# Two reorderings in a graph network kernel: carried sums fetched three blocks ahead, and edge products made between two count batches

## The chip, the cores and the metric

The kernel runs on one core of one Trainium2 chip. The metric is device time in microseconds (us) of one execution, all stages in one launch. The five engines are PE (TensorE), DVE (VectorE), ACT (ScalarE), POOL (GpSimd) and SP (SyncE); here POOL does nearly nothing but issue indirect DMAs (gathers), and SP issues the plain ones.

## The reference

A two-layer graph network over 12,500 nodes and 400,000 edges (sorted by target), cut to what matters:

```python
# first layer
msg = relu(concat([x[dst], x[src], edge_attr, u[dst]]) @ W1 + b1)
agg = segment_sum(msg, dst)
x   = layernorm(x + relu(concat([x, agg, u]) @ W2 + b2))
# second layer, run twice, with a batch norm behind each run
h   = h0 @ W + b                      # per node
msg = h[src] + edge_attr @ We + be    # per edge
h   = batchnorm(relu(segment_sum(msg, dst) + h) + bias)
x   = layernorm(x + h)
```

The second layer's sum over edges is done as a dense product: for blocks of edges the kernel first counts how often each source node occurs (a matrix of counts, `adj`, kept in HBM), and multiplies these counts by the node values.

## The kernel before, in words

**Edge part** (about 165 to 4605 us of the span). The 400,000 edges are 3125 tiles of 128, five tiles to a step, 625 steps. Sixteen steps are a cycle; cycles 2 to 38 of the 39 whole ones also build the count matrices. Each engine runs its own written-out order of a cycle in a loop; semaphores tie them. In step j of a cycle:

- POOL gathers, in `gather_step` (L703), five times 128 rows of `b_tab` (the source's share of the message) into `rows`, which holds eight steps. Five times a cycle it also gathers target rows, `gather_target` (L690). So there are 85 gathers in a cycle.
- PE makes the **edge products** in `before_add` (L835, L836), two f32 matmuls for the step two ahead, into one of two PSUM halves. It waits for `added` of the step that used this half, which is step j.
- DVE adds the products to the gathered rows: `add_step` (L1402). It waits for the products and for the five gathers. SP then stores the rows to `q_tab`.
- DVE makes the one-hot operands of two **count batches**, before and after the add: `make_hot` (L1411, two instructions each). `make_hot` may start when the batch before the last one is done (`built`).
- PE multiplies them in `build_batches` (L852): 16 matmuls for d = 0, 16 for d = 1. ACT copies the counts to SBUF (L1127, `kept`).
- In steps 1, 4, 7, 10 and 13 DVE also runs the **window terms** of one block of 128 windows of 16 edges, `window_terms` (L1416, L1417, L1419; both inputs in SBUF, f32). In the step behind (2, 5, 8, 11, 14) PE sums such a block in two halves of eight matmuls each, `over_turn` (L877), and in the step behind that DVE scans it (L1455).

**Node part** (about 4605 to 5160 us). For each of 98 blocks of 128 nodes POOL gathers a window of edge rows (`gather_window`, L739, five buffers) and one row of carried sums for each node (`gather_carry`, L747). DVE works the window off in `node_term` (L1416, L1417, L1419, and L1425 that ends it), PE sums it in `node_sum` (L936). Seven blocks are a group; `node_sums` (L1532) adds the carried sums, and waits for all seven carried gathers of its group and for PE's seven sums. POOL's window for block b + 5 waits for PE's sum of block b.

**Second layer** (about 5160 to 7700 us): PE multiplies counts by node values (L998), twice, then a short end.

Of the kernel before, what the change touches and what calls it, by code (L numbers as in the profile page):

```python
# [7 lines left out]
STEPS = TILES // S  # L8
NB = -(-N // P)
# [28 lines left out]
CYCLE = 16  # L38
# [2 lines left out]
BUILD = AP_ // 2  # L41
HOT = 8
WIN = 5
BATCH = 4
PAIR_BATCHES = P // BATCH
QH = NB // 2

def build(nc, a, out):
# [3 lines left out]
    with ctx:  # L52
# [127 lines left out]
        a_node = arena(0, (NB, F))  # L180
        win = arena(25088, (WIN, WM, W0))
        at = 50176
# [98 lines left out]
        carried_on = sem("carried_on")  # L281
        win_got = [sem(f"win_got{u}") for u in range(WIN)]
        a_w_in = [sem(f"a_w_in{n}") for n in range(MC)]
# [369 lines left out]
        def _(pool):  # L653
# [16 lines left out]
            for g in range(NG):  # L670
                if g >= 2:
                    pool.wait_ge(rows_compared, g - 1)
                for q in range(GB):
                    b = g * GB + q
# [61 lines left out]
            def gather_window(b):  # L736
                u = b % WIN
                wait(pool, node_summed, b - WIN + 1 if b >= WIN else 0)
                nc.gpsimd.indirect_dma_start(  # L739
# [3 lines left out]
            def gather_carry(b):  # L743
                g, q = b // GB, b % GB
                if g >= 2 and q == 0:
                    pool.wait_ge(agg_made, g - 1)
                nc.gpsimd.indirect_dma_start(  # L747
                    m_carry_in[:, g % 2, q, :], None, m_carry[:, :],
                    bass.IndirectOffsetOnAxis(ap=m_carried[:, b:b + 1], axis=0)).then_inc(m_carry_in_s[g % 2], 16)

            for b in range(WIN):
                gather_window(b)
            pool.wait_ge(m_carry_out, 16 * MOB)
            for b in range(NB):
                gather_carry(b)
                if b + WIN < NB:
                    gather_window(b + WIN)

            for l in range(2):
                pool.wait_ge(a_carry_out[l], 16 * AOP)  # L760
                for i in range(NB // 2):
                    wait(pool, cat_made, i + l * (NB // 2))
                    for h in range(2):
                        b = 2 * i + h
# [11 lines left out]
        def _(pe):  # L776
# [49 lines left out]
            def before_add(c, j):  # L826
                uu, k = j // 2, j % 2
                us, half = uu % 4, k
                m = c * CYCLE + j
                use = c * 2 + uu // 4  # L830
                wait(pe, added, m - 1)
                if k == 0:
                    pe.wait_ge(eat_in[us], use * 16 + 16)
                pe.nop(nofuse=True)
                mm(psum[:, half, 2 * W0:5 * W0], eat[:, us, 1 - k, 0, :], w_edge[:, :], start=True, stop=True)  # L835
                mm(psum[:, half, 0:2 * W0], eat[0:2 * C, us, 1 - k, 1, :], w_edge[0:2 * C, W0:3 * W0], start=True, stop=True)\  # L836
                    .then_inc(pre_done, 1)

            def build_batches(c, j):
                for d in range(2):  # L840
                    n = j * 2 + d
                    s = (c - 1) * (2 * CYCLE) + n
                    pe.wait_ge(hot_made, s + 1)
                    for b in range(2):
                        r = s * 2 + b
                        bank = 2 + 2 * b
                        wait(pe, kept, r * 2 - 2)
                        pe.nop(nofuse=True)
                        for e in range(BATCH):
                            for h in range(2):  # L850
                                at = slice(h * HALF, (h + 1) * HALF)
                                one = mm(psum[:, bank + h, e * NB:(e + 1) * NB], hot_lo[at, d, b * BATCH + e, :],  # L852
                                         hot_hi[at, d, b * BATCH + e, :], start=True, stop=True)
                        one.then_inc(built, 1)
                    over_turn_at(c, j, d)

            def turn_codes():
# [28 lines left out]
            def over_turn_at(c, j, part):  # L886
                if j in (2, 5):
                    if not (isinstance(c, int) and c == 0):
                        over_turn(c * MC - 2 + j // 5, 3 + j // 5, part)
                elif j in (8, 11, 14):  # L890
                    over_turn(c * MC + (j - 8) // 3, (j - 8) // 3, part)
# [10 lines left out]

            def tile_cycle(c, build_now):
                for j in range(CYCLE):
                    if isinstance(c, int) and c * CYCLE + j + 2 >= STEPS:
                        pass
                    elif j + 2 < CYCLE:
                        before_add(c, j + 2)
                    else:
                        before_add(c + 1, j + 2 - CYCLE)  # L910
                    if isinstance(c, int) and c == 0 and j == 8:
                        turn_codes()
                    if build_now:
                        build_batches(c, j)
                    else:
                        over_turn_at(c, j, 0)
                        over_turn_at(c, j, 1)
                    over_back_at(c, j)
# [163 lines left out]
        def _(act):  # L1082
# [33 lines left out]
            def keep_batches(c, j):  # L1116
                for d in range(2):
                    s = (c - 1) * (2 * CYCLE) + (j * 2 + d)
                    for b in range(2):
                        r = s * 2 + b  # L1120
                        at = j * 4 + d * 2 + b
                        h2, column = at // PAIR_BATCHES, at % PAIR_BATCHES * BATCH
                        if column == 0 and not (isinstance(c, int) and c == 1):
# [641 lines left out]
```

## Time and profile before

| | |
|---|---|
| median of the runs before | 7802.66 us (3 runs, 7797.47 to 7810.06) |
| time of the profiled execution | 7799.23 us |
| its span, first to last instruction | 7797.5 us |
| busy in the span | PE 77%, DVE 57%, ACT 27%, POOL 51% |
| mean granted TensorE clock | 0.765 of full speed |
| HBM traffic | 271 GB/s over the span |

The profiled execution's own time is 1.7 us longer than its span, and 3.4 us under the median. How the rows further down are read: a row of a stretch has its bounds, its length, then the busy time of PE, PEld (weight loads), DVE, ACT and POOL, each with its number of instructions, the granted clock, the DMA share and GB/s. A row of a group has the number of instructions, then busy us and mean ns of one, then the engine's idle us just before them and what ended it ("issue": nothing that the profile shows). A row of a waits view has us in total, times and the longest. A row in order of time has start and length in us, and in brackets the idle time before it.

The share of busy time is a mean over stages that have different limits, so the stages have to be looked at one by one: the edge part is more than half of the time, and the change touches it and the node part, not the second layer.

### The profile page before, as it was taken

What the parts mean: (1) busy time and instruction counts of PE and PEld (TensorE: products, weight loads), DVE (VectorE), ACT (ScalarE), POOL (GpSimd) and SP (SyncE); (2) the same over time, 40 slices, a digit from 0 to 9 for tenths busy, and PEclk for the clock granted to TensorE, in tenths of its full rate; (3) what the DMA queues carried; (4) which work ended last, traced back from release to release, by engine and by line L of the source; (5) the groups of instructions that cost most, each with busy time, mean ns of one, the idle gap of its engine ahead of it and who ended that gap; (6) DMA issues with size and microseconds to landing.
All of it is one profiled execution on the core that took longest, in us unless ns stands there. A gap on an engine that the chain in (4) does not pass through costs nothing.

```text
span 7797.5 us, 166429 instructions
## 1 busy us (share of the span) xinstructions
PE 6012.8 (77%) x60257; PEld 5159.6 (66%) x60257; DVE 4425.6 (57%) x5943; ACT 2114.4 (27%) x5348; POOL 3965.5 (51%) x3933
## 2 busy tenths in 40 slices
PE   3177777777777777777777756689999999999996
PEld 3055555555555555555555546679999999999996
DVE  4168888888888888888888848840011111011113
ACT  1044444444444444444444400000000000000001
POOL 7777777777777777777777764410011110001111
PEclk7576666666666666666666666689999999999998
DMA  5157777777777777777777774569999998999996
GB/s 141 49 175 241 249 237 249 246 253 243 241 257 239 249 241 243 257 245 248 240 248 245 253 221 160 162 257 381 362 382 382 383 381 345 381 363 381 384 380 245
DMA packets 973999, 2113.94 MB, mean 271 GB/s; under 512 B 668085, under 2 KB 759691, under 8 KB 860003
## 3 DMA queue, kind: packets, MB, share of 16 engines
q1 hardware_dynamic: 809823, 1841.27, 63.4%
q0 software_dynamic: 136064, 258.22, 13.6%
q10 hardware_dynamic: 28030, 13.36, 0.9%
q8 instruction: 51, 0.84, 0.0%
q14 instruction: 31, 0.25, 0.0%
HBM read 1457.70 MB, written 654.73 MB: 271 GB/s over the span
## 4 chain that ended last, share of the span: by engine, by line
PE 48%; DVE 20%; issue 12%; DMA 10%; POOL 7%; DVEq 1%; SPq 1%; ACTq 0%; ACT 0%; POOLq 0%
PE psum L998 25%; PE psum L877 10%; DVE edge_area L1411 9%; POOL arena L703 5%; PE psum L852 4%; DMA arena<-adj 4%; PE psum L835 4%; PE psum L836 2%; DVE arena L1402 2%; DMA arena<-b_tab,arena 2%; DMA arena<-in_src_steps 2%; DVE edge_area L1416 1%; DVE arena L1419 1%; DVE arena L1416 1%; POOL arena L717 1%
## 5 line engine op out<-in xcount | busy, mean ns | idle before, releaser
L703 POOL DMA_INDIRECT arena<-b_tab,arena x3125 | 3116.1, 997 | 952.6 <-issue 936.4
L1411 DVE TENSOR_TENSOR edge_area<-psum,arena 128x1024 bf16<-128x1024 f32 x2368 | 2487.4, 1092 | 625.0 <-PE psum L852 624.9
L1127 ACT CAST arena<-psum 128x392 bf16<-128x392 f32 x4736 | 1921.0, 505 | 2113.8 <-PE psum L852 2088.0
L998 PE MATMUL psum<-arena 128*128 128x192 bf16 x29008 | 2446.0, 246 | 29.2 <-DMA arena<-adj 20.9
L998 PEld LDWEIGHTS psum<-arena 128*128 128x128 bf16 x29008 | 2400.5, 98 | 38.0 <-issue 35.2
L852 PE MATMUL psum<-edge_area 64*128 64x98 bf16 x18944 | 1226.1, 241 | 464.8 <-ACT arena L1127 456.9
L765 POOL DMA_INDIRECT arena<-a_carry,a_carried x196 | 185.4, 946 | 2397.3 <-DVE arena L1629 1386.6
L835 PE MATMUL psum<-w_edge,arena 96*128 96x288 f32 x1250 | 677.3, 638 | 885.2 <-DVE arena L1402 885.2
L852 PEld LDWEIGHTS psum<-edge_area 64*128 64x128 bf16 x18944 | 782.3, 110 | 711.3 <-issue 683.1
L1595 DVE TENSOR_REDUCE arena<-psum 128x64 f32<-128x192 f32 x296 | 104.2, 352 | 1698.0 <-PE psum L998 1112.6
L835 PEld LDWEIGHTS psum<-w_edge,arena 96*128 96x128 f32 x1250 | 268.7, 268 | 962.3 <-issue 962.3
L877 PE MATMUL psum<-ident,edge_area 128*96 128x128 f32 x3744 | 648.2, 346 | 1.3 <-ACT arena L1132 0.8
L877 PEld LDWEIGHTS psum<-ident,edge_area 128*96 128x96 f32 x3744 | 595.7, 219 | 28.9 <-issue 3.4
L836 PE MATMUL psum<-w_edge,arena 64*128 64x192 f32 x1250 | 547.2, 533 | 0.0
L836 PEld LDWEIGHTS psum<-w_edge,arena 64*128 64x128 f32 x1250 | 271.9, 270 | 397.9 <-issue 397.9
L1213 ACT COPY arena<-psum 98x256 f32<-98x256 f32 x98 | 36.5, 373 | 1622.2 <-PE psum L1022 1622.2
L1402 DVE TENSOR_TENSOR arena<-psum,arena 128x480 f32<-128x480 f32 x625 | 404.7, 648 | 112.8 <-DMA arena<-b_tab,arena 112.6
L877 PE MATMUL psum<-ident,over_area 128*96 128x128 f32 x2528 | 445.6, 350 | 8.4 <-DVE over_area L1419 6.9
L936 PE MATMUL psum<-arena,ident 128*128 128x96 f32 x1568 | 291.0, 363 | 182.3 <-DVE arena L1425 182.1
L877 PEld LDWEIGHTS psum<-ident,over_area 128*96 128x96 f32 x2528 | 407.6, 222 | 27.4 <-issue 10.1
L936 PEld LDWEIGHTS psum<-arena,ident 128*128 128x128 f32 x1568 | 275.0, 272 | 196.6 <-DVE arena L1425 107.4
L1204 ACT COPY arena<-psum 128x128 f32<-128x128 f32 x50 | 13.3, 266 | 890.2 <-PE psum L1015 890.2
(248 smaller groups left out, 3185.3 us busy)
## 6 DMA issues: line engine op xcount, KB each, us to landing
arena<-adj SPq DMA_DIRECT2D x592, 1568.0 KB, 8.8
adj<-arena SPq DMA_DIRECT2D x296, 1568.0 KB
q_tab<-arena SPq DMA_DIRECT2D x312, 480.0 KB
edge_area<-q_tab SPq DMA_DIRECT2D x117, 768.0 KB
arena<-in_edge_t_steps SPq DMA_DIRECT2D x312, 192.0 KB
over_area<-q_tab SPq DMA_DIRECT2D x78, 768.0 KB
arena<-b_tab,arena POOLq DMA_INDIRECT x3125
over_area<-m_cont SPq DMA_DIRECT2D x196, 48.0 KB
```

The source lines that it names most:

```text
L703: nc.gpsimd.indirect_dma_start(rows[:, us, k, S - 1 - s, :], None, b_tab[:, :], bass.IndirectOffsetOnAxis(ap=index[:, us, 1 - k, s:s + 1], ...
L765: nc.gpsimd.indirect_dma_start(a_carry_in[:, h, :], None, a_carry[l][:, :], bass.IndirectOffsetOnAxis(ap=a_carried[:, b:b + 1], axis=0)).t ...
L835: mm(psum[:, half, 2 * W0:5 * W0], eat[:, us, 1 - k, 0, :], w_edge[:, :], start=True, stop=True)
L836: mm(psum[:, half, 0:2 * W0], eat[0:2 * C, us, 1 - k, 1, :], w_edge[0:2 * C, W0:3 * W0], start=True, stop=True)\
L852: one = mm(psum[:, bank + h, e * NB:(e + 1) * NB], hot_lo[at, d, b * BATCH + e, :], hot_hi[at, d, b * BATCH + e, :], start=True, stop=True)
L877: one = mm(psum[0:W0, 7, 0:P], over_win[n % 2][:, i, :], ident[:, :], start=(i == 0), stop=(i == WM - 1))
L936: one = mm(wide_ps(g % 2)[:, q * P:q * P + W0], ident[:, :], win[:, b % WIN, i, :], start=(i == 0), stop=(i == WM // 2 - 1))
L998: one = mm(psum[:, h, 0:3 * F], ring[:, r, n, :], xs[l][:, k, :], start=(k == 0 and not own), stop=(k == NB - 1))
L1127: copy(stage[:, h2, h, :, column:column + BATCH], psum[:, 2 + 2 * b + h, 0:BATCH * NB].rearrange("p (e n) -> p n e", n=NB)).then_inc(kept, 1)
L1402: V.tensor_tensor(of, psum[:, k, 0:S * W0], of, ALU.add).then_inc(added, 1)
L1411: one = V.tensor_tensor(to[:, d, :, :], over(lanes, [P, HOT, n], 1), over(code, [P, HOT, n], 2), ALU.is_equal)
L1416: V.tensor_tensor(of, of, over(target, [P, WM, F], 1), ALU.add).then_inc(targeted, 1)
```

## The change: what it does

Two edits. On POOL, the carried sums of the first three blocks are gathered at once, and from then on the gather of block b + 3 stands where that of block b stood. On PE, in cycles that build counts, the edge products for the step two ahead are made behind the first count batch, instead of ahead of both. What each instruction computes is the same, and so is their number.

```diff
+AHEAD = 3
...
             pool.wait_ge(m_carry_out, 16 * MOB)
+            for b in range(AHEAD):
+                gather_carry(b)
             for b in range(NB):
-                gather_carry(b)
+                if b + AHEAD < NB:
+                    gather_carry(b + AHEAD)
                 if b + WIN < NB:
                     gather_window(b + WIN)
...
+            def edge_products_ahead(c, j):
+                if isinstance(c, int) and c * CYCLE + j + 2 >= STEPS:
+                    pass
+                elif j + 2 < CYCLE:
+                    before_add(c, j + 2)
+                else:
+                    before_add(c + 1, j + 2 - CYCLE)
...
             def build_batches(c, j):
                 for d in range(2):
...
                         one.then_inc(built, 1)
+                    if d == 0:
+                        edge_products_ahead(c, j)
                     over_turn_at(c, j, d)
...
             def tile_cycle(c, build_now):
                 for j in range(CYCLE):
-                    if isinstance(c, int) and c * CYCLE + j + 2 >= STEPS:
-                        pass
-                    elif j + 2 < CYCLE:
-                        before_add(c, j + 2)
-                    else:
-                        before_add(c + 1, j + 2 - CYCLE)
+                    if not build_now:
+                        edge_products_ahead(c, j)
```

On PE, step 5 of a cycle that builds counts (`w_edge,arena` are the edge products, `psum<-edge_area` of 128x98 a count batch, `ident,edge_area` the first half of a window sum), before:

```order
L835 MATMUL psum<-w_edge,arena 128x288 [waits added]
L836 MATMUL psum<-w_edge,arena 128x192
L852 MATMUL psum<-edge_area 128x98 [waits hot_made,kept]
L852 MATMUL psum<-edge_area 128x98 x7
L852 MATMUL psum<-edge_area 128x98 [waits kept]
L852 MATMUL psum<-edge_area 128x98 x7
L877 MATMUL psum<-ident,edge_area 96x128 [waits m_back_kept,masked,relued]
L877 MATMUL psum<-ident,edge_area 96x128 x7
L852 MATMUL psum<-edge_area 128x98 [waits hot_made,kept]
L852 MATMUL psum<-edge_area 128x98 x7
```

The same step with the change (its lines are numbered 4 to 14 higher):

```order
L864 MATMUL psum<-edge_area 128x98 [waits hot_made,kept]
L864 MATMUL psum<-edge_area 128x98 x7
L864 MATMUL psum<-edge_area 128x98 [waits kept]
L864 MATMUL psum<-edge_area 128x98 x7
L839 MATMUL psum<-w_edge,arena 128x288 [waits added]
L840 MATMUL psum<-w_edge,arena 128x192
L891 MATMUL psum<-ident,edge_area 96x128 [waits m_back_kept,masked,relued]
L891 MATMUL psum<-ident,edge_area 96x128 x7
L864 MATMUL psum<-edge_area 128x98 [waits hot_made,kept]
L864 MATMUL psum<-edge_area 128x98 x7
```

The first count batch no longer stands behind the wait for `added`; the edge products now stand behind it and ahead of the window sum.

On POOL, the beginning of the node part (`m_window` are windows, `m_carried` carried sums), before:

```order
L739 DMA arena<-q_tab,m_window 128x1536 x4
L747 DMA arena<-m_carry,m_carried 128x96 [waits m_carry_out]
L739 DMA arena<-q_tab,m_window 128x1536 [waits node_summed]
L747 DMA arena<-m_carry,m_carried 128x96
L739 DMA arena<-q_tab,m_window 128x1536 [waits node_summed]
```

With the change:

```order
L740 DMA arena<-q_tab,m_window 128x1536 x4
L748 DMA arena<-m_carry,m_carried 128x96 [waits m_carry_out]
L748 DMA arena<-m_carry,m_carried 128x96 x3
L740 DMA arena<-q_tab,m_window 128x1536 [waits node_summed]
L748 DMA arena<-m_carry,m_carried 128x96
L740 DMA arena<-q_tab,m_window 128x1536 [waits node_summed]
```

Three more carried gathers stand ahead of the window of block 5; behind that the two kinds alternate as before, the carried ones three blocks on.

## Rows read from the trace of the kernel before

**Rows 1.** Busy time by engine (x instructions) in a stretch of the edge part.
```profile
2000.00:3000.00 1000.00, 727.36 (x6789) 539.05 (x6787) 843.40 (x972) 482.78 (x1221) 762.85 (x778) 0.66 0.76 246
```
**Rows 2.** Groups of instructions on POOL, 950 to 4500 us.
```profile
L703 POOL DMA_INDIRECT arena<-b_tab,arena x2602 | 2556.7, 983 | 793.1 <-issue 778.2 <-DMA arena<-in_src_steps 14.9
```

**Rows 3.** The same view, 511 to 840 us.
```profile
L703 POOL DMA_INDIRECT arena<-b_tab,arena x239 | 239.0, 1000 | 72.8 <-issue 72.5 <-DMA arena<-in_src_steps 0.3
```

**Rows 4.** The same view, 4490 to 4601 us.
```profile
L703 POOL DMA_INDIRECT arena<-b_tab,arena x79 | 79.9, 1012 | 24.1 <-issue 23.8 <-DMA arena<-in_src_steps 0.3
```

**Rows 5.** Waits of DVE, 950 to 4500 us: us in total, times, longest.
```profile
DVE edge_area L1411 <- PE psum L852: 551.1, 519, 1.5
DVE arena L1402 <- DMA arena<-b_tab,arena: 6.2, 1, 6.2
```

**Rows 6.** The same view, 4490 to 4601 us.
```profile
DVE arena L1402 <- DMA arena<-b_tab,arena: 66.9, 15, 10.7
```

**Rows 7.** Instructions of POOL in order of time, 2010 to 2018 us (start, length).
```profile
2011.27 0.94 POOL L703 DMA_INDIRECT arena<-b_tab,arena  x1 [0.30 <-issue]
2012.52 1.16 POOL L703 DMA_INDIRECT arena<-b_tab,arena  x1 [0.30 <-issue]
2013.98 1.44 POOL L703 DMA_INDIRECT arena<-b_tab,arena  x1 [0.30 <-issue]
```

**Rows 8.** Instructions of DVE in order of time, 2007 to 2040 us.
```profile
2011.65 1.22 DVE L1416 TENSOR_TENSOR edge_area<-edge_area,arena 128x1024 f32<-128x1024 f32 x1
...
2016.53 0.65 DVE L1402 TENSOR_TENSOR arena<-psum,arena 128x480 f32<-128x480 f32 x1
...
2020.37 2.11 DVE L1411 TENSOR_TENSOR edge_area<-psum,arena 128x1024 bf16<-128x1024 f32 x2 [1.17 <-PE psum L852]
...
2024.43 2.10 DVE L1411 TENSOR_TENSOR edge_area<-psum,arena 128x1024 bf16<-128x1024 f32 x2 [1.40 <-PE psum L852]
...
2027.72 2.11 DVE L1411 TENSOR_TENSOR edge_area<-psum,arena 128x1024 bf16<-128x1024 f32 x2 [0.61 <-PE psum L852]
...
2032.32 1.21 DVE L1416 TENSOR_TENSOR edge_area<-edge_area,arena 128x1024 f32<-128x1024 f32 x1
```

**Rows 9.** Matmuls of PE in order of time, 2014 to 2030 us.
```profile
2017.33 1.30 PE L835 MATMUL psum<-w_edge,arena 96*128 96x288 f32 x2 [2.30 <-DVE arena L1402]
...
2020.14 3.67 PE L877 MATMUL psum<-ident,edge_area 128*96 128x128 f32 x16
2023.75 0.53 PE L852 MATMUL psum<-edge_area 64*128 64x98 bf16 x16
...
2026.04 0.65 PE L835 MATMUL psum<-w_edge,arena 96*128 96x288 f32 x2
```

**Rows 10.** Instructions of POOL in order of time, 676 to 682 us.
```profile
676.72 1.99 POOL L703 DMA_INDIRECT arena<-b_tab,arena  x1 [0.30 <-issue]
679.01 1.43 POOL L703 DMA_INDIRECT arena<-b_tab,arena  x1 [0.30 <-issue]
```

**Rows 11.** Instructions of DVE in order of time, 676 to 682 us.
```profile
676.67 1.22 DVE L1416 TENSOR_TENSOR over_area<-over_area,arena 128x1024 f32<-128x1024 f32 x1
```

**Rows 12.** Instructions of POOL in order of time, 2098 to 2104 us.
```profile
2101.26 1.43 POOL L703 DMA_INDIRECT arena<-b_tab,arena  x1 [0.31 <-issue]
```

**Rows 13.** Instructions of DVE in order of time, 2098 to 2104 us.
```profile
2100.00 1.26 DVE L1416 TENSOR_TENSOR over_area<-over_area,arena 128x1024 f32<-128x1024 f32 x1
```

**Rows 14.** Waits of DVE in the node part, 4636 to 5150 us.
```profile
DVE edge_area L1532 <- DMA arena<-m_carry,m_carried: 65.2, 13, 9.8
DVE edge_area L1532 <- PE psum L936: 3.4, 1, 3.4
```

**Rows 15.** Instructions of POOL in order of time, 4630 to 4650 us.
```profile
4631.38 1.34 POOL L747 DMA_INDIRECT arena<-m_carry,m_carried  x1 [16.01 <-DMA m_carry<-over_area]
4633.03 1.88 POOL L739 DMA_INDIRECT arena<-q_tab,m_window  x1 [0.30 <-PE psum L936]
```

**Rows 16.** Instructions of DVE in order of time, 4636 to 4660 us.
```profile
4639.01 1.23 DVE L1416 TENSOR_TENSOR arena<-arena 128x1024 f32<-128x1024 f32 x1 [2.11 <-DMA arena<-q_tab,m_window]
```

## The prediction, made before the changed kernel was run

> **What bounds the kernel now.** I read the busy time by stretches first, then the groups on POOL and the waits of DVE in each part, then the order of time. In the edge part PE and DVE are the busiest engines, 727 and 843 of 1000 us, and POOL shows 763 [rows 1]. The reader should look at POOL's idle time next: between 950 and 4500 us its 2602 gathers were busy 2556.7 us and idle 793.1 us, and all that idle time ended by "issue" or by an index load that was there in time [rows 2]. That is 0.30 us before each gather, in the row of each of them [rows 7]. So POOL gathers without a pause: (2556.7 + 793.1) / 2602 = 1.287 us each. The five target gathers of a cycle take 1.25 us, the distance of two undisturbed ones (2011.27 to 2012.52) [rows 7]. A cycle of 80 + 5 gathers thus takes 103.0 + 6.25 = 109.2 us on POOL, with nothing left over.
>
> DVE looks bound by PE: 519 waits for a count batch, 551 us, and a single wait for gathered rows [rows 5]. Both readings hold, because the two are coupled. An undisturbed gather takes 1.25 us, and 85 of them 106.25 us; the other 3.0 us of a cycle are gathers that DVE stretches. With window terms from 2011.65 on [rows 8] the gathers of 2012.52 and 2013.98 took 1.16 and 1.44 us instead of 0.94 to 0.95 [rows 7]: 0.70 us. How much it costs hangs on where in a gather the terms begin. At 0.38 us behind a gather's start it was that 0.70. At 1.25 us behind the last but one gather (terms at 2100.00 [rows 13], gather at 2101.26 [rows 12]) a single gather took 1.43, which is 0.49 more. With a start at 676.67 [rows 11], just ahead of the gather of 676.72, that one took 1.99 and the next 1.43 [rows 10]: 1.04 + 0.49 = 1.53 us. So each of five window terms in a cycle costs POOL between 0.49 and 1.53 us, now 3.0 / 5 = 0.60. POOL cannot go under 106.25 + 5 x 0.49 = 108.7 us for a cycle, nor over 106.25 + 5 x 1.53 = 113.9.
>
> This is why the two have the same pace. If POOL runs ahead, the terms begin later within a gather, and stretch more; if it falls back, less. It settles where the stretch makes its cycle as long as DVE's loop through PE, near the cheap end. The same groups read where that is not so give other paces. At 511 to 840 us, before it has settled: (239.0 + 72.8) / 239 = 1.305 us, 80 x 1.305 + 6.25 = 110.6 us [rows 3]. At 4490 to 4601 us, where no counts are built, DVE waits for gathered rows (15 times, 66.9 us [rows 6]), and the gathers take (79.9 + 24.1) / 79 = 1.316 us, 111.6 us for 85 [rows 4].
>
> The node part is DVE's. Between groups of seven blocks it waited 13 times for carried sums, 65.2 us, and once for PE's last sum of the group, 3.4 us [rows 14].
>
> **The carried sums.** Three gathers move ahead; none is added. A group's last one is issued three blocks earlier, so `node_sums` then waits for what is late next: PE's sum of the seventh block, which starts when DVE has ended that block. The one group in which the carried sums were there already shows that wait, 3.4 us. Groups 2 to 13 waited 65.2 - 9.8 = 55.4 us; 12 x 3.4 = 40.8 stays. Gain: 14.6 us. In the first group the wait of 9.8 would fall by 6.4 to 3.4, but three carried gathers stand ahead of the window of block 5, 1.25 to 1.65 us each from start to start (1.65 for the first [rows 15]). That window was issued at 4633.03 [rows 15], and DVE already waited for it, until 4639.01 [rows 16]; 3.8 to 5.0 us come on top. That leaves 1.4 to 2.6 us; I take 1.9. Where `gather_carry` waits for `agg_made` of two groups before, the window of two blocks into the group is queued behind it; DVE has passed that sum four blocks earlier, so it costs nothing, and up to the 4.6 us per group that are to be won if it did not. Sum of the node part: -16.5 us (bounds -14 and -19 by the first group and the rounding of 3.4).
>
> **The edge products.** Two matmul instructions change places with sixteen in each building step; no DMA moves, and SP, ACT, DVE and POOL keep their order. In three steps DVE now goes from 2011.65 to 2032.32, 20.67 us, with three waits, 1.17, 1.40 and 0.61 us [rows 8]. The first is for the count batch that stands behind the products, which wait for the add of 2016.53 [rows 8, 9]; with the change the batch is made during that add, and the wait goes. The second is for the batch behind the window sum's first half (2020.14, 3.67 us, batch at 2023.75 [rows 9]). Products, batch and window sum are still one after the other, so this batch comes at about the same time and takes over the 1.17 us. The third batch stands behind the products of 2026.04 [rows 9]; without them it comes some 0.85 us earlier, and this is what the three steps win: about 19.7 to 20 us instead of 20.67. In the plain step of a cycle all of its wait (some 1 us) goes. DVE's own loop would then need 109.2 - 5 x 0.8 - 1 = 104 us for a cycle.
>
> That is less than POOL's least, 108.7. So DVE catches up with POOL and waits for gathered rows, and POOL sets the pace alone. What this can win is 109.2 - 108.7 = 0.5 us a cycle. What it costs: nothing keeps the window terms at the cheap end of a gather any more. Where they fall follows the landing of the step's last gather, with SP's stores in the same DMA engines, and so is near to arbitrary. The two stretches in which POOL was not held by DVE's loop had 110.6 and 111.6 us; the bounds are 108.7 and 113.9. I take 110.8, near the first, because counts are built there and not in the second: +1.56 us for each of the (4500 - 950) / 109.2 = 32.5 cycles that are locked now, +51 us. The cycles before 950 us already have this pace and change by nothing; if they fell too, that is 3 x 1.9 us.
>
> The Trainium skill speaks against this price: its page "SBUF — State Buffer", section "Who interferes with whom", says that `tensor_tensor` with both inputs in SBUF contends only with GpSimd's reads, and infers that it leaves descriptor generation alone. By that alone the gathers would not feel the window terms, and the edge part would change by nothing. The trace differs: gathers of 0.94 us became 1.16 to 1.99 beside these terms.
>
> **Sum.** -16.5 + 51 = +34 us on the profiled 7799.2 (of which the span is 7797.5): 7833. The median of the runs shown is 3.4 us above that execution, so 7837 for the median.
>
> **Rivals.**
> 1. POOL's pace stays as it is. The stretch would belong to POOL's own stream, and not to where DVE's terms fall. For it: the row of 950 to 4500 us is one even pace. Against it: the same stream ran at 1.305 and 1.316 us elsewhere [rows 3, 4]. Only the node part counts: -16.5, 7786. The rule of the Trainium skill named above would give the same.
> 2. Faster: DVE waits at the add for undisturbed rows, its terms follow the add by a fixed time, and that time falls at the cheap point of a gather in all five steps. This decides as soon as the five cost less than 3.0 us together. At 0.49 each, 0.54 x 32.5 = 17.5 us are won, with the node part 34: 7769. For it: DVE would be slaved to gathers. Against it: it was at 4490 to 4601 us, and the pace there was the worst.
> 3. Dearer still: as in that stretch, 111.6 us, +2.4 x 32.5 - 16.5 = +61, 7864; at the bound 113.9 it would be +136.
> 4. The carried gathers win nothing because the windows behind them come late in each group: +51 alone, 7854.
>
> **How the numbers follow.** A measurement here can tell about 0.2%, 15.6 us. My forecast, a pace between 110.2 and 111.2 (+16 to +48 us), 0.45; dearer (3 and 4), 0.15; a pace of 109.3 to 110.2, which the node part cancels, 0.12; rival 1, 0.14, which lies at the edge of 0.2%, two thirds of it within; rival 2, 0.14. So slower 0.60, same 0.21, faster 0.19. The range leaves out the lower half of rival 2 and the upper part of 3: 7776 to 7878. The forecast's own range is 7819 to 7851.
>
> **What would show it.** After the change DVE's waits for count batches in the edge part should be far under 551 us, and its waits for gathered rows in the hundreds. POOL's gathers should still idle 0.30 us each; their mean should be over 983 ns, about 1000. With `node_sums` the 13 waits for carried sums should be gone and waits of 3.4 us for PE stand there. I am wrong if the mean gather is at or under 983 ns with DVE waiting for rows (rival 2), if DVE still waits for PE as before (the loop did not get shorter, and the lock holds), or if POOL waits for anything.

## The result, and the profile after

Slower by far more than forecast. The changed kernel takes 7924.29 us (median of 4 runs, 7921.1 to 7928.89); the kernel before took 7801.74 us beside it. The ratio is 1.0158, with an interval of 1.0142 to 1.0174. The prediction was 7837, with a range up to 7878.

The span grew from 7797.5 to 7919.4 us, 121.9 us. In the two traces the last gather of the edge part starts at 4598.24 us before and at 4735.53 after: +137.3 us. From DVE's last add of the edge part to its last `node_sums` it was 544.1 us before and 526.5 after: -17.6 us. The other 2.2 us lie behind that. The loss grows about evenly: the gather that started at 950 us in the trace before comes 15.9 us later, that of 2000 us 50.4 later, that of 3000 us 80.7, that of 4500 us 135.4.

In the changed file the lines are some ten further down: the gathers are L704, target gathers L691, `add_step` L1412, `make_hot` L1421, the window terms L1426, L1427 and L1429, the scan L1465, `build_batches` L864, `node_sums` L1542. The stretch that answers to [rows 1]:

```profile
2000.00:3000.00 1000.00, 704.61 (x6618) 513.11 (x6616) 814.05 (x941) 474.98 (x1188) 770.23 (x755) 0.65 0.74 239
```

All engines but POOL do less in these 1000 us (fewer cycles pass); POOL is busier with fewer instructions, 755 against 778. The groups on POOL from 950 to 4620 us answer to [rows 2]:

```profile
L704 POOL DMA_INDIRECT arena<-b_tab,arena x2600 | 2633.2, 1013 | 792.4 <-issue 792.4
L691 POOL DMA_INDIRECT arena<-a_tab,arena x163 | 196.0, 1202 | 49.7 <-issue 49.7
```

The idle time is the same 0.30 us a gather as before, and nothing else is waited for. But a gather takes 1013 ns instead of 983, and the target gathers 1202. A cycle is 80 x (2633.2 + 792.4) / 2600 + 5 x (196.0 + 49.7) / 163 = 105.4 + 7.5 = 112.9 us, where it was 109.2. The waits of DVE in the same stretch answer to [rows 5]:

```profile
DVE arena L1412 <- DMA arena<-b_tab,arena: 450.8, 234, 6.2
DVE edge_area L1421 <- PE psum L864: 208.4, 126, 2.7
```

DVE's 519 waits for count batches have become 126, and 234 waits for gathered rows stand in their place. In the node part (4741 to 5270 us) the answer to [rows 14] is:

```profile
DVE edge_area L1542 <- PE psum L946: 47.9, 14, 3.9
DVE arena L1426 <- DMA arena<-q_tab,m_window: 6.3, 1, 6.3
```

The waits for carried sums are gone; 14 waits of 3.4 us for PE's last sum of a group stay, and DVE waits 6.3 us for the first group's window where [rows 16] has 2.11.

So far each step reads as predicted. What was not is in POOL's order of time. First around 2009 us:

```profile
2008.23 0.95 POOL L704 DMA_INDIRECT arena<-b_tab,arena  x1 [0.30 <-issue]
2009.48 3.71 POOL L704 DMA_INDIRECT arena<-b_tab,arena  x1 [0.30 <-issue]
2013.49 0.94 POOL L704 DMA_INDIRECT arena<-b_tab,arena  x1 [0.30 <-issue]
```

and DVE at the same time:

```profile
2004.27 0.15 DVE L1463 COPY carry<-over_area 96x1 f32<-96x1 f32 x1 [0.16 <-PE psum L891]
2004.45 0.48 DVE L1465 TENSOR_TENSOR_SCAN over_area<-over_area,carry,psum 96x128 f32<-96x128 f32 x1
2004.85 2.08 DVE L1421 TENSOR_TENSOR edge_area<-psum,arena 128x1024 bf16<-128x1024 f32 x2
2006.84 0.64 DVE L1412 TENSOR_TENSOR arena<-psum,arena 128x480 f32<-128x480 f32 x1
2007.41 2.09 DVE L1421 TENSOR_TENSOR edge_area<-psum,arena 128x1024 bf16<-128x1024 f32 x2
2009.42 1.21 DVE L1426 TENSOR_TENSOR edge_area<-edge_area,arena 128x1024 f32<-128x1024 f32 x1
2010.55 0.68 DVE L1427 TENSOR_TENSOR edge_area<-edge_area,mask_area 128x512 f32<-128x512 f32 x1
2011.16 1.21 DVE L1429 SCALAR_TENSOR_TENSOR edge_area<-edge_area,mask_area 128x1024 f32<-128x1024 f32 x1
```

One gather of 0.94 us lasts 3.71 us: from 0.06 us behind the first term's start to 0.82 us behind the third term's end (2012.37). That is 2.77 us over. Nothing in [rows 7], [rows 10] or [rows 12] looks like this. Now the same phase at another block of the same trace, POOL and then DVE:

```profile
2172.38 1.97 POOL L691 DMA_INDIRECT arena<-a_tab,arena  x1 [0.30 <-issue]
2174.65 1.44 POOL L704 DMA_INDIRECT arena<-b_tab,arena  x1 [0.30 <-issue]
```

```profile
2169.72 0.66 DVE L1412 TENSOR_TENSOR arena<-psum,arena 128x480 f32<-128x480 f32 x1 [0.56 <-DMA arena<-b_tab,arena]
2170.30 2.10 DVE L1421 TENSOR_TENSOR edge_area<-psum,arena 128x1024 bf16<-128x1024 f32 x2
2172.31 1.21 DVE L1426 TENSOR_TENSOR edge_area<-edge_area,arena 128x1024 f32<-128x1024 f32 x1
2173.44 0.68 DVE L1427 TENSOR_TENSOR edge_area<-edge_area,mask_area 128x512 f32<-128x512 f32 x1
2174.05 1.22 DVE L1429 SCALAR_TENSOR_TENSOR edge_area<-edge_area,mask_area 128x1024 f32<-128x1024 f32 x1
```

Here the gather also begins 0.07 us behind the first term, but it ends 0.22 us behind the second (2174.12), and the next one is held to 0.82 behind the third: 1.03 + 0.50 = 1.53 us, the dearest price that the prediction knew, as in [rows 10]. The difference that the reader can see is ahead of the terms: the second time DVE paused at the add, the first time it had run on without a pause since the scan of 2004.45.

Counted over the blocks of the edge part between 440 and 4620 us of the two traces (the price of a block is what the gathers that overlap its terms took over 0.945 us; "held" is one gather over 2.6 us):

| | blocks | held | mean price, held | mean price, others | price in all |
|---|---|---|---|---|---|
| before | 193 | 0 | | 0.63 us | 122 us |
| after | 185 | 77 | 2.19 us (1.68 to 2.93) | 0.79 us (0.47 to 1.52) | 253 us |

The 131 us between the two sums are nearly all of the 137.3 that the edge part lost. Of the 77 held blocks none had a pause of DVE between the last scan and the terms; of the 108 others 105 had one, most of them the wait for rows at the add. Before, 183 of 193 had paused for a count batch at the first `make_hot` of the step, five instructions ahead of the terms.

The kernel before has held gathers too, outside the stretch that is counted here: where no counts are built yet, DVE runs from the scan through the add into the terms. POOL and then DVE in the trace before:

```profile
431.85 3.94 POOL L703 DMA_INDIRECT arena<-b_tab,arena  x1 [0.30 <-issue]
```

```profile
431.07 0.48 DVE L1455 TENSOR_TENSOR_SCAN over_area<-over_area,carry,psum 96x128 f32<-96x128 f32 x1
431.47 0.63 DVE L1402 TENSOR_TENSOR arena<-psum,arena 128x480 f32<-128x480 f32 x1
432.02 1.21 DVE L1416 TENSOR_TENSOR edge_area<-edge_area,arena 128x1024 f32<-128x1024 f32 x1
```

The gather is 2.99 us over. The block before it, at 419.03, held one for 3.03 us, and in the node part the block of 4610.38, right behind a scan, held a window's gather for 3.49.

### The profile page after: what moved, and what is told of

It is laid out like the page before. It is cut to its first block, busy times and chain, and to the rows that moved or that the text cites. A ratio compares the mean times of both kernels' runs of the same rounds, so it can differ in the third digit from the quotient of the medians.

```text
span 7919.4 us, 166429 instructions
## 1 busy us (share of the span) xinstructions
PE 6017.0 (76%) x60257; PEld 5126.8 (65%) x60257; DVE 4414.2 (56%) x5943; ACT 2135.8 (27%) x5348; POOL 4102.1 (52%) x3933
## 4 chain that ended last, share of the span: by engine, by line
PE 36%; POOL 29%; issue 13%; DVE 12%; DMA 9%; SPq 1%; DVEq 1%; ACT 0%; POOLq 0%; ACTq 0%
POOL arena L704 25%; PE psum L1008 25%; PE psum L891 5%; DMA arena<-adj 4%; DVE edge_area L1421 3%; DMA arena<-b_tab,arena 3%; PE psum L864 2%; DVE arena L1429 1%; POOL arena L691 1%; DVE arena L1426 1%; PE psum L839 1%; POOL arena L676 1%; POOL arena L718 1%; DVE arena L1435 1%; PE psum L840 1%
## 5 line engine op out<-in xcount | busy, mean ns | idle before, releaser
L704 POOL DMA_INDIRECT arena<-b_tab,arena x3125 | 3206.6, 1026 | 952.4 <-issue 951.8
L1421 DVE TENSOR_TENSOR edge_area<-psum,arena 128x1024 bf16<-128x1024 f32 x2368 | 2459.6, 1086 | 241.9 <-PE psum L864 235.3
L1137 ACT CAST arena<-psum 128x392 bf16<-128x392 f32 x4736 | 1940.9, 500 | 2224.3 <-PE psum L864 2162.9
L864 PE MATMUL psum<-edge_area 64*128 64x98 bf16 x18944 | 893.7, 238 | 995.4 <-DVE edge_area L1421 832.9
L864 PEld LDWEIGHTS psum<-edge_area 64*128 64x128 bf16 x18944 | 659.1, 112 | 1242.3 <-issue 1200.5
L1412 DVE TENSOR_TENSOR arena<-psum,arena 128x480 f32<-128x480 f32 x625 | 406.7, 651 | 626.2 <-DMA arena<-b_tab,arena 624.8
L891 PE MATMUL psum<-ident,edge_area 128*96 128x128 f32 x3744 | 674.9, 355 | 1.3 <-ACT arena L1142 0.8
L891 PEld LDWEIGHTS psum<-ident,edge_area 128*96 128x96 f32 x3744 | 614.9, 225 | 64.7 <-issue 51.9
L840 PE MATMUL psum<-w_edge,arena 64*128 64x192 f32 x1250 | 527.8, 516 | 0.0
L691 POOL DMA_INDIRECT arena<-a_tab,arena x196 | 230.7, 1177 | 62.6 <-issue 59.4
```

What stands on the lines that cost most here:

```text
L691: nc.gpsimd.indirect_dma_start(a_w[:, n, :], None, a_tab[:, :], bass.IndirectOffsetOnAxis(ap=over_target[:, n:n + 1], axis=0)).then_inc(a_ ...
L704: nc.gpsimd.indirect_dma_start(rows[:, us, k, S - 1 - s, :], None, b_tab[:, :], bass.IndirectOffsetOnAxis(ap=index[:, us, 1 - k, s:s + 1], ...
L891: one = mm(psum[0:W0, 7, 0:P], over_win[n % 2][:, i, :], ident[:, :], start=(i == 0), stop=(i == WM - 1))
L1137: copy(stage[:, h2, h, :, column:column + BATCH], psum[:, 2 + 2 * b + h, 0:BATCH * NB].rearrange("p (e n) -> p n e", n=NB)).then_inc(kept, 1)
L1412: V.tensor_tensor(of, psum[:, k, 0:S * W0], of, ALU.add).then_inc(added, 1)
L1421: one = V.tensor_tensor(to[:, d, :, :], over(lanes, [P, HOT, n], 1), over(code, [P, HOT, n], 2), ALU.is_equal)
```

## The experiments

**The two edits alone.** The first kernel keeps the carried sums ahead and puts the edge products back; the second has the new order of PE and `AHEAD = 0`.

```
-AHEAD = 3
+AHEAD = 0
```

Carried sums alone:

> The carried sums alone, with PE's old order. Theory A (the edge products did the harm, through POOL's gathers): the node part gives its 17.6 us alone, so 7784 us (7779 to 7790) and the edge part keeps its 983 ns per gather. Rival (the new gather order costs something elsewhere, so both edits share the blame): 7800 or more.

Measured: 7783.93 us, ratio 0.9981 (0.9971 to 0.999), -16.4 us. POOL's mean was 982 ns and DVE's waits for PE 537.9 us, 505 times, as before the change.

The order alone:

> The edge products between the two batches alone. Theory A: the whole edge part's 137 us stay, about 7940 us (7930 to 7955), mean gather about 1013 ns or more. Rival (the harm needs both edits): within 20 us of 7802.

Measured: 7948.63 us, ratio 1.02 (1.0183 to 1.0217), +148 us; 76 of 185 blocks held. The whole loss is PE's order, and the carried sums are worth what was predicted. The two do not quite add up to the change's +123; the held blocks fall a little differently in each run of the loop (cycles of 113.15 and 112.93 us).

**Is it the window terms?** Both kernels, with the three terms of the edge part's blocks cut to one of 16 slots, all else and all waits kept:

```
-                V.tensor_tensor(of, of, over(target, [P, WM, F], 1), ALU.add).then_inc(targeted, 1)
+                V.tensor_tensor(of, of, over(target, [P, n, F], 1), ALU.add).then_inc(targeted, 1)
...
+                window_terms(order_of_over(b), over_win[...][:, 0:1, :],
+                             m_mask[:, some(b, 1), 0:1]..., a_w[:, n, :], 1)
```

> The changed kernel, with the window terms of the edge part worked for one slot of sixteen; the other fifteen are left out, so DVE's three instructions are short. Theory A (POOL's gathers set the pace and only these terms stretch them): gathers take 0.95 us, a cycle 106.3 to 107 us, about 7690 us. Rival B (PE's new order makes DVE's loop longer): gathers wait for DVE, idle more than 0.3 us each, and a cycle stays over 108. Rival C (rows land late because SP's stores now meet them): DVE still waits for rows and the gathers keep a mean over 1000 ns, 7900 or more.

> The kernel before, with the same fifteen of sixteen slots left out. Theory A: POOL's pace here too, 106.3 to 107 us a cycle, about 7705 us, so that the order of the edge products is worth nothing once nothing stretches a gather, and the changed kernel with small terms is faster by the node part's 17 us alone. Rival B: faster than the changed kernel with small terms by 30 us or more.

Measured: 7649.94 us (ratio 0.9807, 0.9791 to 0.9824) and 7662.8 us (0.9826, 0.9809 to 0.9842). POOL, in the new order and then in the old one, 950 to 4400 us:

```profile
L704 POOL DMA_INDIRECT arena<-b_tab,arena x2602 | 2457.2, 944 | 792.8 <-issue 791.6 <-DMA arena<-in_src_steps 1.2
```

```profile
L703 POOL DMA_INDIRECT arena<-b_tab,arena x2602 | 2457.2, 944 | 792.8 <-issue 789.1 <-DMA arena<-in_src_steps 3.7
```

Without long terms every gather takes 944 ns in either order, a cycle 106.1 us in both. The last gather of the edge part starts at 4469.78 us in the new order and at 4468.83 in the old one, so the 12.9 us between the two lie behind the edge part. So the order of PE costs nothing by itself: POOL waits for no engine's loop in either. All that the change lost goes through the terms. Both came out some 40 us lower than expected: terms this short hold no gather at all.

**Does a pause ahead of the terms let the gather through?** First by a stricter wait, as the kernel before had it: in the five steps with terms DVE's first count batch waits for PE's last one.

```
-                wait(dve, built, s * 2 - 2)
+                wait(dve, built, s * 2 - (0 if d == 0 and j in (1, 4, 7, 10, 13) else 2))
```

> The changed kernel, with one wait made stricter: in the five steps of a cycle that hold a block of window terms, VectorE's first count batch waits for TensorE's last batch of the step before, so that VectorE pauses a few instructions ahead of the terms, as it did before the change. Nothing is left out. Theory (a gather is held through all three terms only where VectorE ran into them without a pause): the gathers of 2.7 to 3.9 us go, each block of terms costs GpSimd 0.5 to 1.5 us again, a cycle takes 109 to 111 us in place of 112.9, time 7790 to 7870, although VectorE waits more. Rival (the pause has nothing to do with it; the new order of TensorE puts the terms at worse moments of the gathers): the long gathers stay and the time is 7900 to 7950.

Measured: 7897.04 us, ratio 1.0122 (1.0105 to 1.0139). The time misses the theory's range and lies just under the rival's; the trace is the theory's: not one of 186 blocks is held, and the mean price is 0.78 us. But the new wait lengthened the loop of DVE and PE, and POOL now stands still for it. The waits of DVE and those of POOL in this kernel:

```profile
DVE edge_area L1421 <- PE psum L864: 615.8, 306, 2.7
```

```profile
POOL arena L704 <- issue: 816.2, 2405, 4.2
```

The longest idle time before a gather is 4.2 us where it was 0.3, and the cycle 112.55 us for another reason than in the changed kernel. So the pause had to be had without a wait for PE: DVE waits for the end of its own last count batch.

```
+                    if build_now and j in (1, 4, 7, 10, 13):
+                        wait(dve, hot_made, (c - 1) * (2 * CYCLE) + (j * 2 + 2))
                     over_step(c, j)
```

> The changed kernel; ahead of a block of window terms VectorE waits until its own last count batch has ended, a pause of some tenths of a us that hangs on no other engine. Nothing is left out. In the changed kernel 77 of 185 blocks between 440 and 4620 us hold one gather through all three terms and cost GpSimd 2.19 us each, the other 108 cost 0.79 each. Theory (a short pause ahead is enough): no block holds a gather through all three terms, 77 x (2.19 - 0.79) = 108 us come back, time about 7816. Rival (the pause matters only where VectorE waits for another engine, about a us or more): still some 75 held, 7905 to 7935.

Measured: 7824.45 us, ratio 1.0027 (1.0016 to 1.0038). Nearly all the pauses are 0.03 to 0.2 us long, none of 189 blocks is held, the mean price is 0.87 us, the cycle 110.53 us. Some 100 us came back for five short pauses a cycle. Nothing else was moved, so the missing pause is shown to be what made the blocks dear.

**A gap between the terms.** The same kind of wait, behind the second term, and in the next kernel behind the first as well.

```
+                dve.wait_ge(targeted, k + 1)     # in the second kernel only
                 V.tensor_tensor(ea, ea, over(mask, [P, WM, C], 2), ALU.mult).then_inc(masked, 1)
                 dve.wait_ge(targeted, k + 1)
+                dve.wait_ge(masked, k + 1)
```

> The changed kernel; between the second and the third window term VectorE waits until the second has ended (it already waits there for the first), so that the two no longer overlap. Nothing is left out. Theory (a gather gets in wherever VectorE stands still, so a gap between the terms lets a held one go): no gather is held through all three terms, each block costs 0.5 to 1.5 us, time about 7816 (108 us less than the changed kernel). Rival (what decides lies ahead of the terms, in how VectorE came to them): some 75 blocks are still held, 7905 to 7935.

> The changed kernel with such a wait of VectorE on itself behind the first and behind the second window term. Nothing is left out. Theory (a gap lets a held gather go): none is held past the end of the first or second term, the price of a block falls below that of the kernel with one gap; time 7790 to 7816. Rival (what decides lies ahead of the terms): 7905 to 7935.

Measured: 7893.87 us (ratio 1.0115, 1.0099 to 1.0132) and 7970.34 us (1.0217, 1.02 to 1.0234). Both theories missed. A gap does let a held gather go, but the next one is then held by the next term. In the kernel with both gaps, POOL and DVE around 2009 us:

```profile
2009.10 1.60 POOL L704 DMA_INDIRECT arena<-b_tab,arena  x1 [0.30 <-issue]
2011.00 1.86 POOL L704 DMA_INDIRECT arena<-b_tab,arena  x1 [0.31 <-issue]
```

```profile
2008.67 1.21 DVE L1426 TENSOR_TENSOR edge_area<-edge_area,arena 128x1024 f32<-128x1024 f32 x1
2010.02 0.69 DVE L1428 TENSOR_TENSOR edge_area<-edge_area,mask_area 128x512 f32<-128x512 f32 x1
2010.82 1.23 DVE L1431 SCALAR_TENSOR_TENSOR edge_area<-edge_area,mask_area 128x1024 f32<-128x1024 f32 x1
```

The first gather ends 0.82 us behind the first term's end (2009.88), the second 0.82 behind the third's (2012.05). That is 0.66 + 0.92 us for one block; the mean was 1.14 us with one gap and 1.45 with two, where the changed kernel has 1.37 with none.

**Which operand?** The targets and the mask of a block (64 and 16 values a partition) are copied by DVE into PSUM ahead of its step, so that the terms read one input from SBUF and one from PSUM.

```
+                V.tensor_copy(near[:, 0:F], a_w[:, n, :])
+                V.tensor_copy(near[:, F:F + WM], m_mask[...]).then_inc(terms_near, 1)
...
-                window_terms(order_of_over(b), over_win[...], m_mask[...], a_w[:, n, :])
+                    target = near[:, 0:F]
+                    mask = near[:, F:F + WM]
...
+                window_terms(order_of_over(b), over_win[...], mask, target)
```

> The changed kernel, with the small operands of the window terms (64 targets and 16 mask values of a block) copied by VectorE into PSUM a step ahead, so that each of the three terms has one input in SBUF and one in PSUM. Nothing is left out; ten small copies a cycle are added on VectorE. Theory (a gather is held by a VectorE instruction that reads two inputs from SBUF): all gathers take 0.94 to 0.95 us, a cycle 106.3 to 106.8 us, time 7650 to 7690, faster than both kernels. Rival (any long VectorE instruction whose big operand is in SBUF holds the gathers): the gathers keep a mean of about 1010 ns and the time stays at 7900 to 7950. If only a part of the terms holds them: between.

Measured: 7660.29 us, ratio 0.982 (0.9803 to 0.9836): 1.8% faster than the kernel before, 264 us under the changed one, with all of the work done. POOL and DVE's third and first terms:

```profile
L706 POOL DMA_INDIRECT arena<-b_tab,arena x2603 | 2456.7, 944 | 793.3 <-issue 779.6 <-DMA arena<-in_src_steps 9.4 <-DVE arena L1447 4.0
```

```profile
L1431 DVE SCALAR_TENSOR_TENSOR edge_area<-edge_area,psum 128x1024 f32<-128x1024 f32 x98 | 118.4, 1208 | 0.0
L1428 DVE TENSOR_TENSOR edge_area<-edge_area,psum 128x1024 f32<-128x1024 f32 x98 | 118.2, 1206 | 0.2 <-DMA edge_area<-q_tab 0.2
```

The terms are as long as ever (1208 and 1206 ns), and no gather feels them: 944 ns, 106.06 us a cycle. The copies did not put a pause in: 150 of the 193 blocks came from the scan without one, and none held a gather. It is the second input from SBUF, not a long DVE instruction, that holds a gather. With the targets alone in PSUM (the mask terms still read two inputs from SBUF):

> The changed kernel with only the targets of the window terms in PSUM: the first of the three terms reads one input from SBUF, the mask terms still two. Nothing is left out. Theory (each term with two SBUF inputs holds gathers): a block of terms still costs GpSimd something, about two thirds of what the changed kernel pays: gathers of 985 to 1000 ns on average, time 7780 to 7870. Rival (only the first and longest term matters, because it is the one a gather meets first): as with both in PSUM, 7650 to 7690. If the mask terms alone do it: as the changed kernel, 7900 to 7950.

Measured: 7791.76 us, ratio 0.9988 (0.9978 to 0.9997); mean gather 986 ns, 131.7 us over 192 blocks or 0.69 us a block, cycle 109.54 us. That is half of the 1.37 us of all three, but more blocks came from the scan without a pause here (136 of 192, where the changed kernel had 80 of 185). Like with like, the mask terms cost 0.84 us behind the scan and 0.31 otherwise, the three terms 2.14 and 0.79. So all three terms take part, and the mask terms by themselves cost some four tenths of what the three do.

**What the order is worth then.** The operands in PSUM with PE's old order:

> The same operands in PSUM, with the old order of TensorE (both edge products ahead of the two count batches) and the carried sums three blocks ahead. Nothing is left out. Theory: no gather is stretched, but the loop of VectorE and TensorE, which waited for each other 551 us in the kernel before, is now what GpSimd may have to wait for; between 7665 (GpSimd alone still paces, as with the terms cut to one slot, 7662.8 less 16.5 for the carried sums plus the copies) and 7784 (the loop itself takes 109 us a cycle). The difference to the same kernel in the new order is what the order of TensorE is worth once no gather is stretched. Rival (the terms still hold gathers): 7784 or more.

Measured: 7769.27 us, ratio 0.996 (0.9946 to 0.9974). DVE's and POOL's waits:

```profile
DVE edge_area L1420 <- PE psum L866: 510.5, 506, 1.5
```

```profile
POOL arena L706 <- issue: 845.3, 2459, 4.4
```

Every gather takes 944 ns, but POOL waits up to 4.4 us: the loop of DVE and PE alone now makes the pace, 109.09 us a cycle. So in the old order this loop needs 109.1 us, copies included, and in the new one at most 106.06. The change of order gives 109 us (7769.27 - 7660.29) as soon as POOL is not held by the terms.

**The pause, or what stands ahead of it?** All held blocks had the scan in their run without a pause. 13 blocks of step 1 had run ten instructions without a pause, but with no scan among them, and none was held. So the scan was replaced by one multiplication of its two large operands; the sums are then not carried along, and `carry`, the scan's start value, is not read.

```
-                V.tensor_tensor_scan(m_run, m_contb[h], psum[0:W0, 7, 0:P], carry[:, 0:1], ALU.mult, ALU.add)
+                V.tensor_tensor(m_run, m_contb[h], psum[0:W0, 7, 0:P], ALU.mult)
```

> The changed kernel with VectorE's scan of a block's window sums replaced by one multiplication of the same two operands, so that the sums aren't carried along and the result is another one; the number of instructions and all waits stay. In the changed kernel all 77 blocks that held a gather through their three terms had no pause of VectorE between the scan and the terms; of the 105 with a pause behind the scan none did, among them 13 that ran ten instructions without one but had no scan among these. Theory S (the scan, not the length of the run, leaves VectorE so that the next terms hold a gather, until it pauses): no block holds a gather any more though the runs without a pause stay, 0.8 to 0.9 us a block, time 7800 to 7840. Theory L (the length of the run without a pause): some 75 blocks are still held, 7890 to 7930.

Measured: 7837.18 us, ratio 1.0046 (1.0029 to 1.0062). 88 of 188 blocks came from the multiplication into the terms without a pause, and one is held, against 77 of 80 with the scan; the mean price is 0.92 us, the cycle 110.77 us. A block of this kernel at the phase of the one of 2009 us, POOL and DVE:

```profile
1875.46 1.98 POOL L704 DMA_INDIRECT arena<-b_tab,arena  x1 [0.30 <-issue]
1877.74 1.43 POOL L704 DMA_INDIRECT arena<-b_tab,arena  x1 [0.30 <-issue]
```

```profile
1870.58 0.28 DVE L1465 TENSOR_TENSOR over_area<-over_area,psum 96x128 f32<-96x128 f32 x1
1870.81 2.11 DVE L1421 TENSOR_TENSOR edge_area<-psum,arena 128x1024 bf16<-128x1024 f32 x2
1872.83 0.65 DVE L1412 TENSOR_TENSOR arena<-psum,arena 128x480 f32<-128x480 f32 x1
1873.39 2.09 DVE L1421 TENSOR_TENSOR edge_area<-psum,arena 128x1024 bf16<-128x1024 f32 x2
1875.41 1.21 DVE L1426 TENSOR_TENSOR edge_area<-edge_area,arena 128x1024 f32<-128x1024 f32 x1
```

No pause, the same sequence, and the gather ends after 1.98 us instead of 3.71. The scan is what makes the difference, until DVE pauses.

An obvious rival is that any instruction with two SBUF inputs would do, since the multiplication reads only one. The node part of the changed kernel speaks against it. There 42 blocks run without a pause from an addition of two SBUF inputs (L1435) into their terms; in 28 of them a gather starts during the first term, and none lasts over 1.92 us. One of them, POOL and DVE:

```profile
4800.66 1.83 POOL L740 DMA_INDIRECT arena<-q_tab,m_window  x1 [6.04 <-PE psum L946]
```

```profile
4799.58 0.96 DVE L1435 TENSOR_TENSOR arena<-arena 128x768 f32<-128x768 f32 x1
4800.45 1.22 DVE L1426 TENSOR_TENSOR arena<-arena 128x1024 f32<-128x1024 f32 x1
```

Whether it is the scan itself or its start value read from SBUF was not parted.

One sum holds for all of these kernels in which POOL waits for nothing: 106.06 us (no gather stretched) and five prices.

| kernel | mean price of a block, us | 106.06 + 5 x price | measured cycle, us | time, us |
|---|---|---|---|---|
| operands in PSUM | 0 | 106.1 | 106.06 | 7660.29 |
| targets in PSUM | 0.69 | 109.5 | 109.54 | 7791.76 |
| pause ahead of the terms | 0.87 | 110.4 | 110.53 | 7824.45 |
| scan replaced | 0.92 | 110.7 | 110.77 | 7837.18 |
| one gap between terms | 1.14 | 111.8 | 111.80 | 7893.87 |
| the change | 1.37 | 112.9 | 112.93 | 7924.29 |
| two gaps | 1.45 | 113.3 | 113.44 | 7970.34 |

## Why the prediction was right in kind and wrong in size

**POOL sets the pace once DVE's loop is shorter**: right. DVE's waits turned from PE to rows, and POOL's idle time stayed 0.30 us a gather. The loop's length, 104 us by the prediction, was not far off: with the operands in PSUM DVE waited 124.6 us for rows in 32.5 cycles, so 106.06 - 3.8 = 102.2 us is an estimate of it, copies included. That in the kernel before the stretched gathers filled up to the pace of DVE's loop is borne out too: that loop alone needs 109.09 us, with the copies, and the cycle took 109.2.

**The carried sums**: right, -16.4 us by their own run and -17.6 between the traces, where -16.5 was forecast; the waits of 3.4 us are there, 14 times.

**The price of the window terms**: the step that failed. "Each of five window terms in a cycle costs POOL between 0.49 and 1.53 us", and of these bounds I took 110.8 us a cycle, (110.8 - 106.25) / 5 = 0.91 us a block. 77 of 185 blocks cost 1.68 to 2.93 us, over the upper bound, the mean was 1.37, and the cycle 112.93 us. That all cycles together stayed under the bound of 113.9 is a mixture of cheap and dear blocks. The bounds were read from a trace in which DVE nearly always paused between the scan and the terms, because it waited there for PE. In the same trace three of the four blocks without that pause held a gather, for 3.03 to 3.94 us, which is 2.09 to 2.99 over; that breaks the bound of 1.53, and I did not read these rows. I costed the wait that the change removes as time won on DVE, and did not ask what else that wait did: behind a pause, the terms no longer kept a gather to their end. For terms that fall arbitrarily but find no gather held, the value taken was right: 110.53 us with pauses put back and 110.77 with the scan replaced, at 7824 and 7837 us. The 87 us between forecast and result are the held blocks, 77 x (2.19 - 0.91) = 99 us, less what the others cost under the value taken, 108 x (0.91 - 0.79) = 13 us: 86. The cycles ahead of 950 us, which I took as unchanged, lost 15.9 us in the same way.

**The rivals.** The pace did change, so the first falls; with it the rule of the Trainium skill that it rested on, in part. Gathers took 944 ns beside terms with one input in PSUM, and 1013 on average beside the same terms with both in SBUF. The Trainium skill's page "SBUF — State Buffer", section "Who interferes with whom", says that a VectorE instruction with at most one SBUF input outside the two-port modes does not contend with GpSimd; the trace agrees. The Trainium skill's inference there that `tensor_tensor` leaves descriptor generation alone did not carry over to a whole gather, as the prediction used it: the gather also reads its row numbers (the second `arena` in its rows), and no run parts that read from the descriptors. The second rival (faster, cheap points) is refuted by the mean of 1013 ns, the fourth by the carried sums' own run. The third (dearer) was right in its sign, and its bound of +136 us is nearer than my forecast, but its reason was the pace without count batches; the held gathers were in no case.

What stays open is why the scan, until DVE pauses, makes the next terms keep a gather to the end of the third. It is not the only way: with the scan replaced one block, at 458 us, still held a gather for 3.64 us. It also wasn't tried to move the scan behind the terms of its step, which would have moved the waits of PE.

## What to carry to other kernels

Before you remove a wait, ask what other engines get from it: here DVE's wait for TensorE was also the pause behind which its next terms did not keep a gather of POOL to their end, and the order that took it away cost 148 us by itself. A bound read from rows holds only for the conditions that all those rows share, so look for what they share, and in the same trace for the longest such instruction, before you call it a bound. And where POOL paces with indirect DMAs, put the small second operand of DVE's long f32 instructions in PSUM: with that, the same reordering is worth 109 us.

## What the runs showed of the hardware

- A gather of 0.94 us beside DVE instructions with two SBUF inputs lasts until 0.82 us behind the end of one of them (or 0.22 us, where it slips in between the second and third window term), up to 3.94 us beside three window terms. DVE itself is hardly slowed: the first term takes 1213 ns in the changed kernel, and 1206 with its operand in PSUM, where no gather is held.
- After a `tensor_tensor_scan` without a pause of DVE, 77 of 80 blocks of three such instructions held one gather through all three; with a pause in between, here mostly 0.03 to 0.2 us, none of 188. After a `tensor_tensor` with two SBUF inputs, also without a pause, none of 28 that a gather met.
- Short gaps between such instructions do not do what a pause ahead of them does: 1.14 us a block with one gap and 1.45 with two, against 0.87 with a pause ahead and 1.37 with neither.
